# Clearing semaphores on GpSimd after the stage boundary, two sigmoid buffers in the output-maximum pass, and first loads in another order, in a two-layer transformer kernel

## The chip, the cores and the metric

The kernel runs on one core of a Trainium2 chip. The metric is the device time of one execution in microseconds (us). TensorE is called PE in the profile, VectorE DVE, ScalarE ACT, GpSimd POOL and SyncE SP. SP computes nothing here; it issues most of the transfers.

## The reference

Input x is 16 batches of 256 tokens of 512 features; ctx is a context of the same shape. All weights are float32. Four blocks follow one another, each as x = x + block(layernorm(x)):

```python
# 1. cross attention, 16 heads of 64: context rows 0..76 and 77..255 are two separate softmaxes
q = xn @ Wq; out = attend(q, txt @ Wk, txt @ Wv) + attend(q, img @ Wk_ip, img @ Wv_ip)
x = x + out @ Wo + bo
# 2. quantized FFN, 512 -> 1536 -> 512; act_qdq needs the largest absolute value of the whole tensor
xq = act_qdq(xn); up = act_qdq(xq @ dq(w_up).T); gate = act_qdq(xq @ dq(w_gate).T)
gate = act_qdq(gate * fixed_qdq_u16(sigmoid(gate)))
x = x + act_qdq(gate * up) @ dq(w_down).T
# 3. one-head attention over the context: both sides go through (v @ W1.T + b1) @ W2.T + b2
x = x + softmax(proj(xn) @ proj(ctx).T / sqrt(512) + mask) @ ctx
# 4. FFN 512 -> 2048 -> 512, each layer with three routed rank-8 LoRA experts, relu between
x = x + mole(relu(mole(xn, 1)), 2)
```

## The kernel before

The matrix products keep float32 accuracy by splitting each operand into a high part (fp32r, written by ACT with a Copy) and a low part (what is left, written by DVE or POOL with a subtraction); `product` issues three matmuls for one (lines L187 to L189).

The program is a row of stages, each one block in which every engine has its own instruction list, ordered by hand and tied by semaphores. The stages, with the name that prefixes their tiles:

- `c0` makes two constants; `pr` projects the context and prepares normalized x.
- `at` is the cross attention over 128 steps (batch and head pair).
- `pg` and `pu` are the gate and up projections of the quantized FFN over 8 chunks of 512 tokens.
- `om` (`output_maximum`) finds the largest absolute value of gate times up, which the last quantization needs. It runs 48 steps n of 1024 columns. Meanwhile PE folds W1 and W2 of block 3 into one Gram matrix and makes the folded keys from the context.
- `dn` (`down`) requantizes and multiplies with w_down, 8 chunks of six steps s.
- `ma` is the masked attention over 16 batches, `lf` the LoRA FFN over 8 chunks.

A stage owns a `Phase`, which hands out tiles and semaphores. When the last engine of a stage has arrived at the barrier at the end of its block, `Phase.__exit__` opens one more block, in which SP clears every semaphore of the phase (L87 to L91), and ends it with a second barrier. The numbers of semaphores are: c0 2, pr 34, at 57, pg 53, pu 29, om 49, dn 16 (and then qf, the phase around pg to dn, 3 in a block of its own), ma 61, lf 35, 339 together.

**Head of at.** ACT first waits for the bias bo and converts it (L932, L933); DVE first waits for that and makes its low part (L852, L853). Only then come their loops, from s = -3: ACT copies the keys (`keys_high`) and the first query projection (`high_parts`, L929), DVE makes the low part (L824), and PE may start the next queries. SP issues the loads of bo after those of xT, k and v.

**om.** DVE's step n is `outputs(n)` (L1665), `products(n + 2)` (L1653), sometimes `context_low` (L1658), and `largest(n)` (L1669); in even steps `rounded` (L1643) comes first. `products` multiplies the gate by its rounded sigmoid `sq`. For even n the sigmoid is computed again by ACT (L1553), for odd n it is loaded from HBM. All loads of `sq` have one buffer, and SP issues them behind the load of raw:

```python
if n >= 2: sp.wait_ge(up_ready, n - 1)
sp.dma_start(raw[:, n % 2, :], ...)
if n % 2:
    if n >= 2: sp.wait_ge(prod_done, n - 1)
    sp.dma_start(sq[:, 1, :], ...)
```

ACT's step n is `products(n)` (up, L1560, and gate, L1562), then side work, among it `context(x)` (L1571), which takes a transposed half chunk of the context, `turn(x)` of PE (L1738), out of PSUM. DVE's `context_low(x)` follows it, and PE's `turn(x + 1)` waits for that. Halves 0 and 1 are done at ACT's n = 3 and 9, DVE's n = 4 and 10; half 2 follows at ACT's n = 15. ACT's `keys` of the first chunk come at n = 16. POOL loads half 2 only after its work on the folded matrices. At the end SP issues five loads of w_down's parts into `wd`, three of them (k 0 to 3, low part, and k 4 to 7, both parts) after the last store of key biases.

**Head of dn.** SP loads the residual of a chunk (`dn_y`, L1822, 1 MB), then raw of step 0, 1 and so on (L1825, 512 KB each). Then ACT makes up (L1850), DVE the product (L1872), ACT oq and the high part (L1853, L1861), DVE the low part (L1874), and PE its first matmul. PE needs `wd` k 4 to 7 from step s = 2 on. POOL stores the results.

**Head of ma.** SP's order is x(0), keys(0), x(1), values(0), mask, the key biases `traw`, and so on. ACT's list has `keys_high(0)`, then a wait for `traw` and its high part (L2174), then `normalized(0)` (L2129), which lets PE start. DVE makes the low part of `traw` (L2113) after `statistics(0)`.

**Head of lf.** POOL clears the tile `zg` in three memsets (L2455 to L2458); DVE and PE begin with `wait_ge(cleared, 3)`. SP loads the first rows of x3, DVE's first work is `stats` (L2473).

Of the kernel before, what the change touches and what calls it, by code (L numbers as in the profile page):

```python
# [23 lines left out]
P = 128  # L24
# [47 lines left out]
class Phase:  # L72


    def __init__(self, nc, name):
        self.nc, self.name, self.ctx = nc, name, ExitStack()
        self.sems, self.blocks = [], ExitStack()
# [25 lines left out]
    def sem(self, name):  # L103
        self.sems.append(self.ctx.enter_context(self.nc.semaphore(f"{self.name}_{name}")))
        return self.sems[-1]
# [17 lines left out]
def kernel_program(nc, a, out):  # L123
# [11 lines left out]
    with ExitStack() as top:  # L135
# [7 lines left out]
        with Phase(nc, "lo") as ph:  # L143
            sides = LoraSides(nc, ph)
            masked_attention(nc, a, ctx_in, keys_d, bias_d, split_d, x2, x3, sides, ident, neghalf)
            lora_ffn(nc, a, sides, x3, out_f, ident, neghalf)

# [81 lines left out]
def cross_attention(nc, a, x_in, ctx_in, x1, xt_d, wg_d, big, scal, ident, neghalf):  # L229
# [3 lines left out]
    with Phase(nc, "xo") as top:  # L233
# [351 lines left out]
def attend_pairs(nc, a, x_in, xn_d, k_d, v_d, x1, xt_d, wq, wo, big, scal, ident, neghalf):  # L585
# [12 lines left out]
    with Phase(nc, "at") as ph:  # L598
# [59 lines left out]
        with nc.Block() as block:  # L658
# [136 lines left out]
            def _(dve):  # L795
# [85 lines left out]
            def _(act):  # L881
# [159 lines left out]
SUB = 6  # L1041
# [125 lines left out]
def quantized_ffn(nc, a, ctx_in, x1, xt_d, wg_d, x2, raw_up, raw_gate, keys_d, bias_d, big, scal, ident, neghalf):  # L1167
# [4 lines left out]
    with Phase(nc, "qf") as top:  # L1172
        with ExitStack() as gates:
            with Phase(nc, "qu") as mid:
                wu = mid.sb("wu", [P, 2, KD, FF], F32R)
                with Phase(nc, "qg") as low:
# [12 lines left out]
            down(nc, x1, x2, raw_up, gate, wd, wd_late, scal, neghalf)  # L1189
# [247 lines left out]
def output_maximum(nc, a, ctx_in, keys_d, bias_d, raw_up, gate, sq_d, big, scal, folds, wd, wd_parts, wd_late, ident):  # L1437
# [9 lines left out]
    with Phase(nc, "om") as ph:  # L1447
# [3 lines left out]
        sq = ph.sb("sq", [P, 2, SC], U16)  # L1451
# [5 lines left out]
        sq_ready, sig_ready, sq_done = ph.sem("sq_ready"), ph.sem("sig_ready"), ph.sem("sq_done")  # L1457
# [49 lines left out]
        with nc.Block() as block:  # L1507
            def place(n):
# [1258 lines left out]
```

## Time and profile before

| | |
|---|---|
| runs | 3504.18 us, median of 3 (3500.18 to 3504.94) |
| profiled execution | 3504.39 us, of which the span from first to last instruction is 3502.7 us |
| mean granted clock of PE | 0.963 of full speed |
| busy, share of the span | PE 92%, DVE 55%, ACT 44%, POOL 22% |
| transfers | 503.48 MB, 144 GB/s mean |

A profile row of the timeline gives the start in us, the duration, the engine (SPq, ACTq: its queue of DMA issues), the line, the operation, output and inputs with their shapes, how many were merged, and in brackets the idle time of the engine before it with what ended it. The row of an issue has the time of issuing, not of the transfer. The semaphore clears themselves have no row: they show as the gap between the last row of a stage and the first of the next.

### The profile page before, as it was taken

The numbers are of one execution on the slowest core, as the hardware profiler recorded it, in microseconds if no ns is written. First come the engines' busy times: TensorE is split into PE (matmuls) and PEld (weight loads), VectorE is DVE, ScalarE is ACT, GpSimd is POOL, SyncE is SP. The second block draws the span as 40 slices with busy tenths as digits, with TensorE's granted clock in tenths as the row PEclk, the third lists the DMA queues.
The fourth block names the chain that finished last, engine by engine and source line by source line (L and its number), as shares of the span: only waits on it lengthen the run. The fifth ranks groups of instructions, "written<-read, shape, count | busy, mean of one in ns | idle before, by whom it ended". The sixth has DMA issues, their size and how long they took to land. (4 is left out here: it accounts for less than half of the span.)

```text
span 3502.7 us, 51565 instructions
## 1 busy us (share of the span) xinstructions
PE 3225.8 (92%) x17304; PEld 2762.2 (79%) x17304; DVE 1919.8 (55%) x3294; ACT 1557.3 (44%) x2948; POOL 779.3 (22%) x1136
## 2 busy tenths in 40 slices
PE   7999979999999979998996787997959999999998
PEld 6989869999999967886885565885847777877776
DVE  3245558888888855556888885554743222122211
ACT  3222257777777743335776775654722111111110
POOL 0000057777777740000000200002710000000000
PEclk9999989999999999999998898998979999999999
DMA  6477754555555426555666675444832100011000
GB/s 184 134 238 235 220 171 148 153 156 165 154 153 159 144 95 243 177 174 174 221 221 218 208 235 200 166 168 148 253 103 84 37 31 19 24 36 37 31 25 12
DMA packets 370165, 503.48 MB, mean 144 GB/s; under 512 B 58940, under 2 KB 237420, under 8 KB 366032
## 3 DMA queue, kind: packets, MB, share of 16 engines
q1 hardware_dynamic: 356746, 475.46, 43.2%
q0 software_dynamic: 4480, 16.78, 1.4%
q10 hardware_dynamic: 8720, 8.41, 0.7%
q8 instruction: 127, 2.08, 0.3%
q14 instruction: 92, 0.75, 0.1%
HBM read 292.86 MB, written 174.11 MB: 133 GB/s over the span
## 5 line engine op out<-in xcount | busy, mean ns | idle before, releaser
L2522 DVE SCALAR_TENSOR_TENSOR lf_hT<-lf_hb,lf_hT 128x512 fp32r<-128x512 f32 x128 | 88.6, 692 | 618.8 <-ACT lf_hT L2587 617.4
L2587 ACT ACTIVATE lf_hT<-lf_hb 128x512 fp32r<-128x512 f32 x128 | 76.8, 600 | 685.1 <-PE lf_py L189 636.4
L770 POOL TENSOR_TENSOR at_prob<-at_prob,at_rec 128x308 f32<-128x308 f32 (+1 forms) x256 | 261.4, 1043 | 199.1 <-DVE at_rec L812 198.9
L906 ACT ACTIVATE at_prob<-at_sc,at_nm 128x77 f32<-128x77 f32 (+1 forms) x1024 | 293.5, 383 | 3.3 <-DVE at_nm L799 3.3
L799 DVE TENSOR_REDUCE at_nm<-at_sc 128x4 f32<-128x308 f32 (+1 forms) x256 | 164.8, 686 | 82.4 <-PE at_sc L960 80.8
L919 ACT ACTIVATE at_pT<-at_tp 128x1024 fp32r<-128x1024 f32 x128 | 131.8, 1030 | 166.7 <-PE at_tp L970 166.6
L187 PE MATMUL lf_hb<-lf_xT,lf_w 128*128 128x512 f32 x512 | 204.8, 400 | 0.0
L189 PE MATMUL lf_hb<-lf_xT,lf_w 128*128 128x512 f32 x512 | 203.7, 398 | 0.0
L189 PE MATMUL lf_py<-lf_w,lf_hT 128*128 128x512 f32 x512 | 203.2, 397 | 0.0
L188 PE MATMUL lf_hb<-lf_xT,lf_w 128*128 128x512 f32 x512 | 203.1, 397 | 0.0
L187 PE MATMUL lf_py<-lf_w,lf_hT 128*128 128x512 f32 x512 | 202.8, 396 | 0.0
L188 PE MATMUL lf_py<-lf_w,lf_hT 128*128 128x512 f32 x512 | 202.3, 395 | 0.0
L187 PE MATMUL dn_py<-qf_wd,dn_om 128*128 128x512 f32 x384 | 150.7, 393 | 25.2 <-DVE dn_om L1874 25.2
L805 DVE TENSOR_REDUCE at_sums<-at_prob 128x4 f32<-128x308 f32 (+1 forms) x256 | 172.9, 676 | 0.0
L816 DVE TENSOR_TENSOR at_pT<-at_tp,at_pT 128x1024 fp32r<-128x1024 f32 x128 | 156.5, 1222 | 29.9 <-ACT at_pT L919 29.9
L187 PE MATMUL pg_bank<-pg_xs,qg_wg 128*128 128x512 f32 x384 | 153.0, 398 | 20.7 <-DVE pg_xs L1369 20.7
L757 POOL TENSOR_TENSOR at_ks<-at_kr,at_ks 128x512 fp32r<-128x512 f32 x128 | 165.3, 1292 | 16.1 <-ACT at_ks L913 16.1
L187 PE MATMUL pu_bank<-pu_xs,qu_wu 128*128 128x512 f32 x384 | 150.8, 393 | 17.4 <-DVE pu_xs L1369 16.9
L2462 POOL TENSOR_SCALAR lf_var<-lf_mv 128x1 f32<-128x1 f32 x32 | 7.1, 223 | 717.4 <-DVE lf_mv L2475 717.4
L187 PE MATMUL at_vq<-at_xT,xo_Wq 128*128 128x256 f32 x512 | 147.0, 287 | 19.3 <-DMA at_xT<-xn_parts 12.7
L187 PE MATMUL at_vq<-at_pT,at_vs 128*128 128x256 f32 x512 | 154.9, 303 | 0.2 <-DVE at_qst L824 0.2
L960 PEld LDWEIGHTS at_sc<-at_ks,at_qs 128*128 128x128 f32 x1024 | 140.4, 192 | 14.2 <-DMA at_qs<-at_qst 4.4
(324 smaller groups left out, 9510.0 us busy)
## 6 DMA issues: line engine op xcount, KB each, us to landing
at_kr<-k_rows SPq DMA_DIRECT2D x256, 128.0 KB, 2.9
at_qs<-at_qst SPq DMA_DIRECT2D x512, 64.0 KB, 2.1
raw_gate<-pg_stage SPq DMA_DIRECT2D x96, 256.0 KB, 2.0
pu_rg<-raw_gate SPq DMA_DIRECT2D x96, 256.0 KB
raw_up<-pu_stage SPq DMA_DIRECT2D x96, 256.0 KB, 2.1
om_raw<-raw_up SPq DMA_DIRECT2D x48, 512.0 KB, 4.3
dn_raw<-raw_up SPq DMA_DIRECT2D x48, 512.0 KB, 3.8
xn_parts<-pr_xturned SPq DMA_DIRECT2D x32, 512.0 KB, 4.8
```

Source lines behind the costliest of these rows:

```text
L187: pe.matmul(out, lh, rh, start=start, stop=False, **kw)
L188: pe.matmul(out, lh, rl, start=False, stop=False, **kw)
L189: return pe.matmul(out, ll, rh, start=False, stop=stop, **kw)
L757: pool.tensor_tensor(ks[:, n % NK, :, 1, :], kr[:, n % NKR], ks[:, n % NK, :, 0, :].bitcast(F32), ALU.subtract).then_inc(k_low, 1)
L770: ins = pool.tensor_tensor(prob[:, i, :, lo:hi], prob[:, i, :, lo:hi], rec[:, z, g, :].unsqueeze(2).broadcast_to([P, 2 * NTE, hi - lo]), A ...
L799: ins = dve.tensor_reduce(nm[:, n % 2, g, :], sc[n % 2][:, :, lo:hi], AX_X, ALU.max, negate=True)
L805: dve.tensor_reduce(sums[:, z, g, :], prob[:, i, :, SEG[g][0]:SEG[g][1]], AX_X, ALU.add).then_inc(sum_done, 1)
L816: dve.tensor_tensor(pT[:, n % 2, 1], tp[:], pT[:, n % 2, 0].bitcast(F32), ALU.subtract).then_inc(pt_done, 1)
L906: ins = act.activation(prob[:, i, m, lo:hi], sc[n % 2][:, m, lo:hi], ACT.Exp, bias=nm[:, n % 2, g, m:m + 1])
L919: act.activation(pT[:, n % 2, 0], tp[:], ACT.Copy).then_inc(pt_hi, 1)
L960: ins = pe.matmul(sc[n % 2][:, h * NTE + m, :], qs[:, n % NQ, h, m * P:(m + 1) * P], ks[:, n % NK, h, part, :], start=part == 0, stop=part ...
L2522: dve.scalar_tensor_tensor(hT[:, i, 1, :], hb[i][:], 0.0, hT[:, i, 0, :].bitcast(F32), ALU.max, ALU.subtract).then_inc(h_done, 1)
```

## The change

Four things are edited.

1. `Phase`: there is no second block. After the barrier of a stage POOL alone gets the clears, ahead of its own list of the next stage, and the other engines go on. The numbers of the semaphores stay taken until the next stage has ended.
2. `om`: `sq` has three buffers, one for even and two for odd n. The load of an odd sq stands ahead of that of raw and waits only for the product four steps back. `turn`, `context` and `context_low` of half 0 move to after PE's beta products, ACT's n = 9 and DVE's n = 10; those of half 1 to after PE's constants, ACT's n = 14 and DVE's n = 15. The load of w_down's k 4 to 7 leaves `om`.
3. `dn`: that load (two of 1 MB) is issued by POOL as soon as raw of step 1 has landed; the residual is loaded after raw of step 1 instead of ahead of step 0.
4. Heads: in `at` bo is converted at s = 0 (ACT) and s = 1 (DVE). In `ma` `traw` is the first load and is split first on ACT and DVE, and its store is issued ahead of the mask.

```diff
     def __exit__(self, *a):
         self.blocks.close()
-        if self.sems:
-            with self.nc.Block() as block:
-                @block.sync
-                def _(sp):
-                    for s in self.sems:
-                        sp.sem_clear(s)
+        if self.leaf:
+            Phase.retired.close()
+        for s in self.sems:
+            self.nc.gpsimd.sem_clear(s)
+        Phase.retired.push(self.sem_ctx.pop_all())
         return self.ctx.__exit__(*a)
...
 # attend_pairs, DVE and ACT
-                dve.wait_ge(bo_high, 1)
-                dve.tensor_tensor(bo[32:64, :], xn[32:64, :], bo[32:64, :].bitcast(F32), ALU.subtract).then_inc(bo_low, 1)
                 for s in range(FIRST, LAST + 1):
+                    if s == 1:
+                        dve.wait_ge(bo_high, 1)
+                        dve.tensor_tensor(bo[32:64, :], xn[32:64, :], bo[32:64, :].bitcast(F32), ALU.subtract).then_inc(bo_low, 1)
...
-                act.wait_ge(bo_ready, 32)
-                act.activation(bo[:], xn[:], ACT.Copy).then_inc(bo_high, 1)
                 for s in range(FIRST, LAST + 1):
+                    if s == 0:
+                        act.wait_ge(bo_ready, 32)
+                        act.activation(bo[:], xn[:], ACT.Copy).then_inc(bo_high, 1)
...
 # output_maximum
-        sq = ph.sb("sq", [P, 2, SC], U16)
+        sq = ph.sb("sq", [P, 3, SC], U16)
...
                 def load_main(n):
+                    if n % 2:
+                        if n >= 4:
+                            sp.wait_ge(prod_done, n - 3)
+                        sp.dma_start(sq[:, place_of(n), :], part(sq_d, n // SUB, n % SUB)).then_inc(sq_ready[n // 2 % 2], 16)
                     if n >= 2:
                         sp.wait_ge(up_ready, n - 1)
                     sp.dma_start(raw[:, n % 2, :], part(raw_up, n // SUB, n % SUB)).then_inc(raw_ready[n % 2], 16)
-                    if n % 2:
-                        if n >= 2:
-                            sp.wait_ge(prod_done, n - 1)
-                        sp.dma_start(sq[:, 1, :], part(sq_d, n // SUB, n % SUB)).then_inc(sq_ready, 16)
...
                 load_down((1,), (0, KD))
-                load_down((0, 1), (KD, 2 * KD))
...
-                    if n == 3:
-                        context(0)
...
                     if n == 9:
...
-                        context(1)
+                        context(0)
...
                         act.activation(bb[:], tb[:, 16:17], ACT.Copy, scale=SCALE).then_inc(gc_out, 1)
+                        context(1)
...
-                    if n == 4:
+                    if n == 10:
                         context_low(0)
-                    if n == 10:
+                    if n == 15:
                         context_low(1)
...
 # down
-                        sp.wait_ge(y_free, 2 * it + par + 1)
-                        sp.dma_start(y[:, par], tokens(x1, 2 * it + par)).then_inc(res_ready[par], 16)
                         for s in range(SUB):
                             sp.wait_ge(up_ready, 2 * SUB * it + SUB * par + s + 1)
                             sp.dma_start(raw[:, s % 2, :], part(raw_up, 2 * it + par, s)).then_inc(raw_ready[s % 2], 16)
+                            if s == 1:
+                                sp.wait_ge(y_free, 2 * it + par + 1)
+                                sp.dma_start(y[:, par], tokens(x1, 2 * it + par)).then_inc(res_ready[par], 16)
...
+                pool.wait_ge(raw_ready[1], 16)
+                for h in range(2):
+                    pool.dma_start(wd[:, h, KD:2 * KD, :].bitcast(F32), wd_parts[:, h, KD:2 * KD, :].bitcast(F32)).then_inc(wd_late[1], 16)
...
 # masked_attention, SP
+            sp.dma_start(traw[:], bias_d.rearrange("c (b s) -> (c b) s", b=NB)).then_inc(traw_ready, 16)
             load_x(0)
             load_keys(0)
             load_x(1)
             load_values(0)
+            sp.wait_ge(t_low, 1)
+            sp.dma_start(split_d, tsplit[:].bitcast(F32)).then_inc(t_stored, 16)
             sp.dma_start(mask[:], a["fside_1xSxS2_0"].rearrange("o (m p) s -> p (o m) s", p=P)).then_inc(m_ready, 16)
-            sp.dma_start(traw[:], bias_d.rearrange("c (b s) -> (c b) s", b=NB)).then_inc(traw_ready, 16)
```

## Rows read from the trace of the kernel before

**Rows 1.** Busy us (and count) of PE, PEld, DVE, ACT, POOL; clock; DMA share; GB/s.

```profile
452.80:1299.20 846.40, 817.64 (x6048) 772.54 (x6048) 662.86 (x1218) 587.48 (x1601) 609.17 (x931) 0.99 0.50 150
1887.20:2125.10 237.90, 180.20 (x760) 136.82 (x760) 204.43 (x190) 173.21 (x191) 30.70 (x32) 0.86 0.72 226
```

**Rows 2.** Timeline, last and first rows around two boundaries.

```profile
1.59 0.29 POOL L159 TENSOR_SCALAR_AFFINE_SELECT ident<-ident 128x128 f32<-128x128 f32 x1 [0.50 <-POOL ident L157]
2.73 0.44 SPq L358 DMA_DIRECT2D pr_rows<-in_ctx_dram  x1
...
1884.68 0.21 DVE L1209 TENSOR_SCALAR scal<-scal 128x1 f32<-128x1 f32 x1
1887.21 0.34 SPq L1516 DMA_DIRECT2D om_raw<-raw_up  x1
```

**Rows 3.** Timeline, head of at.

```profile
462.67 0.63 ACT L933 ACTIVATE at_bo<-at_xn 128x512 fp32r<-128x512 f32 x1 [19.40 <-DMA at_xn<-in_L_xattn_bo_dram]
...
463.72 0.36 ACT L929 ACTIVATE at_qst<-at_vq 128x256 fp32r<-128x256 f32 x1
...
464.60 0.39 PE L187 MATMUL at_vq<-at_xT,xo_Wq 128*128 128x256 f32 x1 [3.64 <-DVE at_qst L824]
```

**Rows 4.** Waits of DVE in om: us in total, times, longest.

```profile
DVE om_prod L1653 <- DMA om_sq<-gate_sigmoids: 27.1, 12, 10.1
```

**Rows 5.** Timeline of om: its head, and the steps 15 and 16.

```profile
1900.65 1.23 DVE L1653 TENSOR_TENSOR om_prod<-qf_gate,om_sq 128x1024 f32<-128x1024 int16 x1 [10.11 <-DMA om_sq<-gate_sigmoids]
...
1965.32 1.23 DVE L1665 TENSOR_TENSOR om_outp<-qf_gate,om_up 128x1024 f32<-128x1024 int16 x1
...
1970.44 1.23 DVE L1665 TENSOR_TENSOR om_outp<-qf_gate,om_up 128x1024 f32<-128x1024 int16 x1 [1.03 <-ACT qf_gate L1562]
...
1967.31 1.02 ACT L1571 ACTIVATE qf_wd<-om_ctp 128x1024 fp32r<-128x1024 f32 x1 [4.33 <-PE om_ctp L1738]
...
1965.33 1.94 PE L1738 MATMUL om_ctp<-ident,om_cin 128*128 128x128 f32 x8 [18.45 <-issue]
```

**Rows 6.** Timeline, boundary from om to dn.

```profile
2129.48 0.40 SPq L1822 DMA_DIRECT2D dn_y<-x  x1
2130.15 15.52 SPq L1825 DMA_DIRECT2D dn_raw<-raw_up  x4
2139.38 1.15 ACT L1850 ACTIVATE dn_up<-dn_raw,scal 128x1024 int16<-128x1024 f32 x1 [18.35 <-DMA dn_raw<-raw_up]
...
2145.54 0.79 PE L187 MATMUL dn_py<-qf_wd,dn_om 128*128 128x512 f32 x1 [25.22 <-DVE dn_om L1874]
```

**Rows 7.** Landing times of the tiles dn_raw, then qf_wd.

```profile
DMA to landing us min/median/max: 3.5/3.8/9.7
...
DMA to landing us min/median/max: 4.7/7.5/9.6
```

**Rows 8.** Windows of dn, columns as in the first group.

```profile
2145.50:2151.50 6.00, 5.96 (x15) 4.66 (x16) 3.40 (x3) 3.44 (x4) 0.00 (x0) 0.52 0.39 96
2151.50:2409.20 257.70, 257.70 (x1138) 213.38 (x1137) 129.48 (x122) 148.47 (x137) 5.48 (x7) 1.00 0.43 147
```

**Rows 9.** Timeline, head of ma.

```profile
2425.49 0.20 POOL L2035 TENSOR_TENSOR ma_shift<-ma_minus,ma_rstd 128x2 f32<-128x2 f32 x1
...
2427.35 0.42 ACT L2174 ACTIVATE ma_tsplit<-ma_traw 16x256 fp32r<-16x256 f32 x1 [2.56 <-DMA ma_traw<-key_biases]
2427.67 1.51 ACT L2129 ACTIVATE ma_xn<-ma_y,ma_shift,ma_rstd 128x512 f32<-128x512 f32 x2
```

**Rows 10.** Timeline, head of lf.

```profile
2581.08 0.53 POOL L2455 MEMSET lf_zg<- 128x512 f32 x1 [27.99 <-POOLq L87]
...
2581.66 0.10 POOL L2457 MEMSET lf_zg<- 128x4 f32 x1
2581.70 0.11 POOL L2458 MEMSET lf_zg<- 128x4 f32 x1
...
2584.05 0.69 DVE L2473 BATCH_NORM_STATS2 lf_st<-lf_xin 128x6 f32<-128x512 f32 x1 [10.11 <-DMA lf_xin<-x]
```

More of the change, by code:

```diff
@@ L72, with __init__ @@
 class Phase:
-    def __init__(self, nc, name):
-        self.nc, self.name, self.ctx = nc, name, ExitStack()
+    retired = ExitStack()
+    def __init__(self, nc, name, leaf=True):
+        self.nc, self.name, self.leaf, self.ctx, self.sem_ctx = nc, name, leaf, ExitStack(), ExitStack()
         self.sems, self.blocks = [], ExitStack()
@@ L103, in sem @@
     def sem(self, name):
-        self.sems.append(self.ctx.enter_context(self.nc.semaphore(f"{self.name}_{name}")))
+        self.sems.append(self.sem_ctx.enter_context(self.nc.semaphore(f"{self.name}_{name}")))
         return self.sems[-1]
@@ L142, in kernel_program @@
         quantized_ffn(nc, a, ctx_in, x1, xt_d, wg_d, x2, raw_up, raw_gate, keys_d, bias_d, big, scal, ident, neghalf)
-        with Phase(nc, "lo") as ph:
+        with Phase(nc, "lo", leaf=False) as ph:
             sides = LoraSides(nc, ph)
@@ L146, in kernel_program @@
             lora_ffn(nc, a, sides, x3, out_f, ident, neghalf)
+    Phase.retired.close()
 def consts(nc, ident, neghalf):
@@ L232, in cross_attention @@
     v_d = nc.dram_tensor("v_rows", (TOK, INNER), F32).ap()
-    with Phase(nc, "xo") as top:
+    with Phase(nc, "xo", leaf=False) as top:
         wq = top.sb("Wq", [P, 2, KD * INNER], F32R)
@@ L1170, in quantized_ffn @@
     sq_d = nc.dram_tensor("gate_sigmoids", (NCH, P, KF * CT), U16).ap()
-    with Phase(nc, "qf") as top:
+    with Phase(nc, "qf", leaf=False) as top:
         with ExitStack() as gates:
-            with Phase(nc, "qu") as mid:
+            with Phase(nc, "qu", leaf=False) as mid:
                 wu = mid.sb("wu", [P, 2, KD, FF], F32R)
-                with Phase(nc, "qg") as low:
+                with Phase(nc, "qg", leaf=False) as low:
                     wg = low.sb("wg", [P, KF, 2, KD, P], F32R)
@@ L1456, in output_maximum @@
         raw_ready = [ph.sem(f"raw_ready{i}") for i in range(2)]
-        sq_ready, sig_ready, sq_done = ph.sem("sq_ready"), ph.sem("sig_ready"), ph.sem("sq_done")
+        sq_ready = [ph.sem(f"sq_ready{i}") for i in range(2)]
+        sig_ready, sq_done = ph.sem("sig_ready"), ph.sem("sq_done")
         up_ready, prod_done, gate_ready, out_done, max_done = (
@@ L1507, in output_maximum, with place_of @@
         with nc.Block() as block:
+            def place_of(n):
+                return 1 + n // 2 % 2 if n % 2 else 0
             def place(n):
@@ L1647, in products @@
                     if s:
-                        dve.wait_ge(sq_ready, 16 * (n // 2) + 16)
+                        dve.wait_ge(sq_ready[n // 2 % 2], 16 * (n // 4) + 16)
                     else:
@@ L1652, in products @@
                         dve.wait_ge(gate_ready, n - 1)
-                    dve.tensor_tensor(prod[:, s, :], place(n), sq[:, s, :], ALU.mult).then_inc(prod_done, 1)
+                    dve.tensor_tensor(prod[:, s, :], place(n), sq[:, place_of(n), :], ALU.mult).then_inc(prod_done, 1)
                 def context_low(x):
@@ L1746, in _ @@
                     ins.then_inc(turned, 1)
-                turn(0)
                 pe.wait_ge(w1_ready, 16)
@@ L1758, in _ @@
                 ins.then_inc(beta_full, 1)
-                turn(1)
+                turn(0)
                 pe.wait_ge(m_out, KD)
@@ L1771, in _ @@
                 ins.then_inc(gc_full, 1)
+                turn(1)
                 pe.wait_ge(gram_low, KD)
@@ L1793, in _, with down @@
                     ins.then_inc(t_full, 1)
-def down(nc, x1, x2, raw_up, gate, wd, wd_late, scal, neghalf):
+def down(nc, x1, x2, raw_up, gate, wd, wd_parts, wd_late, scal, neghalf):
     NO = 3
@@ L2102, in outputs @@
                     dve.scalar_tensor_tensor(y[:, b % NX, t, :], po[:, t, :], rec[:, b % 2, t:t + 1], y[:, b % NX, t, :], ALU.mult, ALU.add).then_inc(y_done, 1)
+            dve.wait_ge(t_high, 1)
+            dve.tensor_tensor(tsplit[:, 1, :], traw[:], tsplit[:, 0, :].bitcast(F32), ALU.subtract).then_inc(t_low, 1)
             for s in range(FIRST, LAST + 1):
@@ L2110, in _ @@
                     statistics(s + 3)
-                if s == FIRST:
-                    dve.wait_ge(t_high, 1)
-                    dve.tensor_tensor(tsplit[:, 1, :], traw[:], tsplit[:, 0, :].bitcast(F32), ALU.subtract).then_inc(t_low, 1)
                 if 0 <= s < B:
@@ L2165, in turned_high @@
                 act.activation(pT[:, b % 2, 0], tp[b % 2][:], ACT.Copy).then_inc(pt_high, 1)
+            act.wait_ge(traw_ready, 16)
+            act.activation(tsplit[:, 0, :], traw[:], ACT.Copy).then_inc(t_high, 1)
             for s in range(FIRST, LAST + 1):
@@ L2171, in _ @@
                     keys_high(s + 2)
-                if s == FIRST + 1:
-                    act.wait_ge(traw_ready, 16)
-                    act.activation(tsplit[:, 0, :], traw[:], ACT.Copy).then_inc(t_high, 1)
                 if 0 <= s + 1 < B:
```

4 lines of the change are left out of this document (1 added, 3 removed).

## The prediction

> **What bounds the kernel now.** I read the page first: PE is busy 92% of the span, every other engine much less. That is an average over stages, so the second view is the table of busy time by stage. In the attention stage PE is busy 817.6 of 846.4 us, so nothing inside its loop can give much, only its head. The output-maximum stage om is another case: DVE is busy 204.4 of 237.9 us, PE 180.2, ACT 173.2 [rows 1]. There DVE sets the pace, and the view of waits says what it misses: 27.1 us in 12 waits, all for the loaded sigmoids, the longest 10.1 us at the head, so 17.0 us in 11 waits later [rows 4]. The third view is the timeline at each boundary between stages, where no engine computes and every microsecond is on the path. The gap from the last row to the first of the next stage is 2.73 - 1.88 = 0.85 us after c0 with 2 semaphores, and 1887.21 - 1884.89 = 2.32 us after pu with 29 [rows 2]. The difference, 1.47 us for 27 more clears, is 0.054 us each; I use 0.055. What is left of 0.85 after two clears, 0.74, is two block exits, 0.37 each.
>
> **Part 1, the clears.** On SP all 339 are on the path. Leaving out ma and lf, which are special, 2 + 34 + 57 + 53 + 29 + 49 + 19 = 243 clears go, 13.4 us, and 8 second exits (qf has its own), 3.0 us: 16.3 us in all (rounded once). The cover is POOL's idle time at the head of each stage. POOL's next work is not on the path after c0, pg, at and dn; after pr it clears tiles for which SP asks late; after pu it issues a context load that PE needs only at n = 9 now. Clears on POOL have no row. Bounds for one: 0.04 us, two memsets in a row at 2581.66 and 2581.70, and 0.11 us, the duration of the shorter kind [rows 10]. I take 0.07, between them and a little above SP's.
>
> After ma POOL is on the path. DVE and PE of lf wait for its memsets, which take from 2581.08 to 2581.81, 0.7 us. The barrier would release at 2581.08 - 61 x 0.055 - 0.37 - about 0.2 = 2577.1; then 61 x 0.07 = 4.3 us of clears and 0.7 of memsets end at 2582.1, while the rows of x, loaded 3.7 us earlier, have landed at about 2580.3. DVE starts at 2582.1 instead of 2584.05 [rows 10]: 1.9 us, between 3.7 (0.04 each) and 0. At the end of the program 35 clears only change engine: 35 x 0.015 = 0.5 us lost and 0.37 won, nothing.
>
> **Part 2, om.** The wait for sq comes from its place: it is issued behind raw, which waits for ACT's up two steps back. Now it is issued about one step earlier, more than the longest but two of the later waits need. Bounds: none of the 17.0 us, if ACT or PE becomes the bound, or all. DVE's busy time leaves room for all (237.9 - 204.4 = 33.5 idle), PE has 57 us of idle. The load of 1 MB at n = 24 still stands in front of one sq. I take 80%, 13.5 us. At the head sq of step 1 now goes ahead of raw of step 1; 512 KB at the stage's 226 GB/s [rows 1] is 2.3 us, and ACT needs raw too, so I take 1.7, between 0 and 2.3.
>
> The moved context half costs. PE's transpose of half 2 must wait for DVE's low part of half 1, which now stands in step 15. DVE has one such operation less ahead of it, so `outputs(15)` comes 1.2 us earlier, at 1964.1; it, `products(17)` and the low part take 3.45 us, to 1967.6. PE's transposes at this slow clock take 1.9, to 1969.5, where ACT had started its copy at 1967.31 and DVE's `outputs(16)` had already waited 1.03 us for what ACT does behind it [rows 5]. So step 16 is 2.2 us late. The low bound of this loss is 0, if POOL's load of half 2 was late anyway by as much (the bracket of PE's row says it was ready just then); the high one 3.5. om gains 13.5 + 1.7 - 2.2 = 13.0 us.
>
> **Part 3, dn.** Raw of step 0 was issued at 2130.15, used at 2139.38: 9.2 us, where the median load of this tile lands in 3.8 [rows 6, 7]. In front of it stood three loads of w_down and the residual. Two of the three and the residual go, so it lands in 3.8: 5.4 us; and the issue of the residual, 2130.15 - 2129.48 = 0.67 us, is no longer ahead. From ACT's first row PE follows 6.2 us later as before, and is busy without a break until 2409.2 [rows 6, 8], so the 6.1 us are kept. What is late next? The two loads on POOL. With R the issue of raw 0, raw 1 has landed at about R + 4.2. PE starts at R + 10.0. Its steps 0 and 1 are 48 matmuls: 15 in 6.0 us at a granted clock of 0.52, 33 at 257.7 / 1138 = 0.226 us [rows 8], 13.5 us, so w_down's second third is needed at R + 23.5. Loads of this kind landed in 7.5 us, 9.6 at worst [rows 7]: side by side R + 12 to 14, one after the other at worst R + 23.4. Hidden, with nothing to spare in the worst case. Raw 2 shares the engines with 3 MB, but is needed only 5 us and more after it is asked for.
>
> **Part 4, heads.** In at PE's first group ended at 464.60 - 3.64 = 460.96. ACT copied the query at 463.72 because the bias came first, at 462.67 [rows 3]. It could start at 461.0: 2.7 us at most. The copies of the bias, 0.63 and 0.68 us, now fall into the filling loop, where ACT and DVE are less covered; I take 2.2, between 0 and 2.7. In ma the start of `normalized(0)` was 2427.67, behind the split of traw, though its shift was ready at 2425.69 [rows 9]. Now traw is long there; but its issue stands ahead of x(0), 0.47 us. So beyond the boundary's 1.9 us the head gains 2427.67 - 2425.69 - 0.47 = 1.5, bounds 0 and 2.0; I take 1.4.
>
> **Sum.** 16.3 + 1.9 (lf) + 13.0 + 6.1 + 2.2 + 1.4 = 40.9 us. From the profiled execution's 3504.4, which stands 0.2 above the median of the runs, that gives 3463.5, so 3464.
>
> **Rivals.** A: the wait in om only changes its name. ACT is busy 173 us and waits for PE's transposes besides [rows 1, 5]; if that loop sets the pace once sq is there, only 4 of the 13.5 us come: 3473. For it: ACT's row at 1967.31 waited 4.33 us for PE. Against it: DVE hardly waits for ACT now, and both others are less busy than DVE.
>
> B: the loads on POOL come late, and PE stalls at s = 2 of the first chunk. It decides from R + 23.5 on. If they need 30 us, the loss is 6.5 us: 3470. For it: 3 MB are under way at once. Against it: the rows of landing above.
> On this the Trainium skill speaks against the change (DMA: Bandwidth & Descriptors, SWDGE vs HWDGE vs iDMA): GpSimd writes its descriptors into SBUF itself, and VectorE locks it out there in its two-port mode, while transfers from SP are immune. No row here shows such a lockout. By the same page's fit (Anatomy of one DMA) a load of 1 MB takes an estimated 4.4 us, and this rival would be dead.
>
> C: the gap at a boundary is not the clears but transfers and the barrier. Then part 1 gives only the exits, 3 us, and the sum is 27: 3477. Against it: the gap grows with the number of semaphores at a steady rate.
>
> D, slower: a clear on POOL is dear, and POOL holds back the heads. Its place is lf (61 ahead of the memsets), the end (35) and at (34 ahead of the clearing of xn, which SP asks for about 5 us in). With c us each the change loses 61c - 6.25 in lf, 35c - 2.3 at the end and 34c - 5 in at, against 39 us won elsewhere; it turns at c = 0.4. At 0.5 it loses 13 us: 3517. Against it: ten times what the rows of small POOL operations show.
>
> **Chances.** The sum as it stands, 3455 to 3468: 0.62. A 0.17, B 0.08, C 0.04, D 0.03. Better than the sum, 3448 to 3455, if om gives all and the heads their upper bounds (3.5 + 2.2 + 0.6 + 0.5 + 1.8 us more): 0.06. The range 3453 to 3480 takes in A, B and C's better part and most of the bounds: the low ones together would give some 30 us less, but not all at once. A difference of 0.2%, 7 us, is about what a measurement of this kernel can tell from none. Faster 0.95, same 0.02, slower 0.03.
>
> **What the profile after would show.** The gap after c0, pr, at, pg, pu and om is about 0.5 us whatever the number of semaphores, and DVE's first row of lf comes 5 us after the last store's landing at most. The waits for sq in om fall from 27 to under 12 us, with one wait of 2 to 3 us more at step 16. ACT's first row of dn comes about 4 us after the issue of raw, and PE has no idle time in dn behind its first row. PE's second group in at starts within 1 us of the end of the first. The prediction is wrong if ACT's or PE's waits in om grow by what DVE's lose, if PE stalls about 13.5 us into dn, or if POOL's first rows come late by more than 0.1 us a semaphore.

## The result, and the profile after

The changed kernel takes 3467.47 us, the median of 4 runs (3466.56 to 3467.89), where the one before takes 3503.55 beside it: 36.1 us less, a ratio of 0.9899 (95% interval 0.9884 to 0.9915). Forecast were 3464 and 40.2 us less than the first median. The profiled execution took 3467.41 us with a span of 3465.7. Two executions stand far off the others of their kernel, one of the sigmoid buffers alone further down (4520.73 us at a mean granted clock of 0.67, the one whose profile was taken) and one of the kernel before beside it (9628.20 us); they are in no time and no ratio below.

The rows answer to those of before, view by view. First the busy table of the stages at and om, with the columns of [rows 1]:

```profile
456.60:1297.80 841.20, 816.53 (x6048) 771.91 (x6048) 664.27 (x1219) 586.57 (x1601) 610.25 (x932) 0.99 0.51 150
...
1876.80:2099.30 222.50, 176.01 (x760) 132.93 (x760) 203.00 (x186) 172.48 (x191) 32.22 (x32) 0.87 0.74 242
```

In om DVE has the same 203 us of work, in 222.5 us. The stretch of om in [rows 1] ends 1.0 us behind its last reduction; cut like this one it is 236.9 us long, so 14.4 us are gone.

The timeline around the first boundary and that from pu to om, as in [rows 2]:

```profile
1.60 0.29 POOL L162 TENSOR_SCALAR_AFFINE_SELECT ident<-ident 128x128 f32<-128x128 f32 x1 [0.50 <-POOL ident L160]
...
2.37 1.84 SPq L361 DMA_DIRECT2D pr_rows<-in_ctx_dram  x5
...
1876.03 0.21 DVE L1214 TENSOR_SCALAR scal<-scal 128x1 f32<-128x1 f32 x1
1876.73 0.34 SPq L1529 DMA_DIRECT2D om_raw<-raw_up  x1
```

Both gaps are now 0.48 and 0.49 us, with 2 semaphores and with 29: where no store is under way, the gap no longer depends on the number.

The view of waits for om, DVE, which answers to [rows 4], and three rows of the timeline at steps 15 and 16, which answer to [rows 5]:

```profile
DVE om_prod L1660 <- DMA om_sq<-gate_sigmoids: 9.7, 2, 8.5
...
DVE om_outp L1672 <- ACT qf_gate L1570: 4.6, 2, 3.5
```

```profile
1955.99 1.94 PE L1745 MATMUL om_ctp<-ident,om_cin 128*128 128x128 f32 x8 [15.20 <-DVE qf_wd L1665]
...
1957.96 1.02 ACT L1579 ACTIVATE qf_wd<-om_ctp 128x1024 fp32r<-128x1024 f32 x1 [7.97 <-PE om_ctp L1745]
...
1961.10 1.23 DVE L1672 TENSOR_TENSOR om_outp<-qf_gate,om_up 128x1024 f32<-128x1024 int16 x1 [3.53 <-ACT qf_gate L1570]
```

Of the waits for sq 1.2 us are left behind the head. The moved context half shows as a chain: PE's transpose waits for DVE's low part, ACT waits 7.97 us for PE, and DVE 3.53 us for ACT, where it had waited 1.03.

The head of dn (timeline), which answers to [rows 6], and the landing times of dn_raw and then of qf_wd, as in [rows 7]:

```profile
2101.31 0.95 SPq L1830 DMA_DIRECT2D dn_raw<-raw_up  x2
...
2105.47 1.15 ACT L1861 ACTIVATE dn_up<-dn_raw,scal 128x1024 int16<-128x1024 f32 x1 [9.22 <-DMA dn_raw<-raw_up]
...
2106.90 1.28 POOL L1839 DMA_DIRECT2D qf_wd<-wd_parts  x2 [7.69 <-DMA dn_raw<-raw_up]
...
2111.63 0.79 PE L190 MATMUL dn_py<-qf_wd,dn_om 128*128 128x512 f32 x1 [16.09 <-DVE dn_om L1885]
```

```profile
DMA to landing us min/median/max: 3.5/3.8/7.2
...
DMA to landing us min/median/max: 7.7/9.1/10.5
```

Raw of step 0 is used 4.2 us after its issue instead of 9.2. POOL's two loads land 7.7 and 10.5 us after theirs, the last of them at about 2118; by the working of rival B PE needs it at 2101.3 + 23.5 = 2124.8. In the table of windows PE has no idle time there, as before it [rows 8]:

```profile
2111.70:2117.70 6.00, 6.00 (x16) 4.72 (x17) 3.28 (x3) 3.54 (x4) 0.00 (x0) 0.55 0.98 371
2117.70:2375.60 257.90, 257.87 (x1138) 213.20 (x1136) 129.49 (x122) 148.26 (x137) 6.07 (x8) 1.00 0.45 146
```

Last the three other heads, from the timeline; they answer to [rows 3, 9, 10]:

```profile
459.08 0.58 PE L190 MATMUL at_vq<-at_xT,xo_Wq 128*128 128x256 f32 x1 [11.67 <-DMA at_xT<-xn_parts]
...
462.05 0.38 ACT L933 ACTIVATE at_qst<-at_vq 128x256 fp32r<-128x256 f32 x1 [0.72 <-PE at_vq L192]
...
462.95 0.58 PE L190 MATMUL at_vq<-at_xT,xo_Wq 128*128 128x256 f32 x1 [0.94 <-DVE at_qst L827]
...
2384.63 0.42 ACT L2178 ACTIVATE ma_tsplit<-ma_traw 16x256 fp32r<-16x256 f32 x1 [23.72 <-DMA ma_traw<-key_biases]
...
2390.51 0.20 POOL L2046 TENSOR_TENSOR ma_shift<-ma_minus,ma_rstd 128x2 f32<-128x2 f32 x1
...
2390.83 1.52 ACT L2139 ACTIVATE ma_xn<-ma_y,ma_shift,ma_rstd 128x512 f32<-128x512 f32 x2 [1.07 <-POOL ma_shift L2046]
```

```profile
2540.81 0.83 SPq L2421 DMA_DIRECT2D lf_xin<-x  x2
...
2545.31 0.53 POOL L2464 MEMSET lf_zg<- 128x512 f32 x1 [29.00 <-issue]
...
2546.06 0.69 DVE L2482 BATCH_NORM_STATS2 lf_st<-lf_xin 128x6 f32<-128x512 f32 x1 [8.91 <-POOL lf_zg L2467]
```

In at PE waits 0.94 us between its first two groups instead of 3.64. In ma ACT normalizes at once when the shift is there. In lf DVE now waits for POOL, whose memsets start 4.5 us after SP's first issue, behind 61 clears.

### The profile page after: what moved, and what is told of

Same layout as the page of the kernel before. It is cut to its first block and busy times, and to the rows that moved or that the text cites. A ratio compares the mean times of both kernels' runs of the same rounds, so it can differ in the third digit from the quotient of the medians.

```text
span 3465.7 us, 51456 instructions
## 1 busy us (share of the span) xinstructions
PE 3221.9 (93%) x17304; PEld 2759.2 (80%) x17304; DVE 1922.2 (55%) x3294; ACT 1554.9 (45%) x2948; POOL 781.9 (23%) x1138
## 5 line engine op out<-in xcount | busy, mean ns | idle before, releaser
L190 PE MATMUL pg_bank<-pg_xs,qg_wg 128*128 128x512 f32 x384 | 153.2, 399 | 16.4 <-DVE pg_xs L1374 16.4
L760 POOL TENSOR_TENSOR at_ks<-at_kr,at_ks 128x512 fp32r<-128x512 f32 x128 | 165.8, 1296 | 11.3 <-ACT at_ks L917 11.3
L191 PE MATMUL pg_bank<-pg_xs,qg_wg 128*128 128x512 f32 x384 | 150.8, 393 | 0.0
```

Source lines behind the costliest of these rows:

```text
L190: pe.matmul(out, lh, rh, start=start, stop=False, **kw)
L191: pe.matmul(out, lh, rl, start=False, stop=False, **kw)
L760: pool.tensor_tensor(ks[:, n % NK, :, 1, :], kr[:, n % NKR], ks[:, n % NK, :, 0, :].bitcast(F32), ALU.subtract).then_inc(k_low, 1)
```

## The experiments

Each kernel was timed beside the one before, on the same chip within a group. The profile of each is one execution, so the stretches are compared over all of them. In the tables of this section "PE's part" of a stage is the time from PE's first row in it to its last.

**The clears alone**, edit 1 on the kernel before.

```diff
-                    for s in self.sems:
-                        sp.sem_clear(s)
+        for s in self.sems:
+            self.nc.gpsimd.sem_clear(s)
```

> The kernel before with the clears alone moved to GpSimd. My theory (the clears and the second exits are on the path, and POOL's clears are covered everywhere but in front of lf): 16.3 + 1.9 = 18.2 us faster than before, each gap between stages shorter by 0.055 us a semaphore and some 0.4 for the exit, lf by about 1.2 to 1.9. Rival C (the gap is transfers and barrier): some 3 us only. Rival D (dear clears): slower. Where the head of at or a projection's first loads become late because SP's clears had covered something, a boundary's gain is missing at PE's first matmul, although it is there at the first issue.

Measured: 3484.11 us against 3500.8, ratio 0.9947 (0.9934 to 0.9961), so 16.7 us by the medians and 18.6 by the ratio (13.7 to 23.1). Rivals C and D are out. With 13 profiles the boundaries can be averaged: five with the clears on SP (before, and the kernels below with edit 3 alone, the heads alone, the buffers alone and the load behind raw) and eight with the clears on POOL. The time from the start of PE's last row of a stage to SP's first issue of the next, in us:

```
into      semaphores  on SP   on POOL   gain   by 0.055 each + 0.37 an exit
at            34       7.92     6.82    1.10      2.24
pg            57       9.37     5.57    3.80      3.51
pu            53       9.50     5.93    3.56      3.29
om            29      12.39    10.55    1.83      1.96
dn            49       9.85     6.21    3.65      3.06
ma         16 + 3      9.11     7.72    1.39      1.78
```

With 0.36 us after c0 (2.73 - 2.37) that is 15.7 us, forecast 16.3. Only the boundary into at misses a whole microsecond. The trace holds the start of each clear and of each wait of SP, though no view prints them, and there the two parts come apart. From the release of the barrier to SP's first issue in at it takes 2.27 us with the clears on SP and 0.08 with them on POOL: 2.19 of the 2.24 are there. But SP arrives at the barrier 3.9 to 4.3 us behind its last issue of pr in the five executions, and 5.0 to 5.5 in the eight, since before that it waits for pr's last stores to land. Why they land 1.1 us later is open.

The same starts show what a clear takes: they stand 0.055 us apart on SP, with one pause of 0.39 us into pg and one of 0.38 into dn, and 0.071 apart on POOL, with one pause each of 0.36 to 0.44 us into at, pg and lf. In the kernel with the clears alone too, DVE's first row of lf waits for POOL:

```profile
2563.70 0.84 SPq L2415 DMA_DIRECT2D lf_xin<-x  x2
...
2568.20 0.53 POOL L2458 MEMSET lf_zg<- 128x512 f32 x1 [29.05 <-issue]
...
2568.96 0.69 DVE L2476 BATCH_NORM_STATS2 lf_st<-lf_xin 128x6 f32<-128x512 f32 x1 [8.95 <-POOL lf_zg L2461]
```

**The sigmoid buffers alone.**

```diff
-        sq = ph.sb("sq", [P, 2, SC], U16)
+        sq = ph.sb("sq", [P, 3, SC], U16)
...
                 def load_main(n):
+                    if n % 2:
+                        if n >= 4:
+                            sp.wait_ge(prod_done, n - 3)
+                        sp.dma_start(sq[:, place_of(n), :], ...)
```

> The kernel before with the two buffers for the loaded sigmoids and their load ahead of raw, and nothing else: the context halves stay at n = 3 and 9, all loads of w_down stay in om. My theory: om is shorter by 17 us or a little less (the changed kernel's om became 14.4 us shorter, and its move of the context halves cost some 2.5 of what the buffers gave); 15 to 17 us faster than before. Rival: the move of the halves cost nothing, and this kernel gains 14.4 or less.

Measured: 3487.92 us against 3500.8, ratio 0.9964 (0.9951 to 0.9978), 12.9 us by the medians and 12.6 by the ratio. The 15 to 17 expected are missed. By the number the rival's 14.4 or less came, but its reason, that the move of the halves cost nothing, falls further down; the 17 us were those of one execution. The kernel was run once more, for a profile of the stage.

> The kernel before with the two sigmoid buffers alone, once more, since the first profile of it was taken at a clock of 0.67. Three profiles of om as it stood before show PE's part of it 223.7, 218.2 and 218.3 us long, with 17.0, 11.2 and 11.3 us of DVE's waits for sq behind the head. My theory: this kernel's waits for sq fall to 1 or 2 us behind the head, and PE's part is 208 to 210 us long, some 9 to 10 below 218.3 and as short as in the changed kernel with the halves back. 11 to 13 us faster than before.

Measured: 3490.77 us against 3501.34, ratio 0.9968 (0.9956 to 0.9980), 10.6 us by the medians, where 11 to 13 were expected. PE's part of om is 209.1 us, as expected. DVE's waits for sq in om, 2.4 us of them behind the head:

```profile
DVE om_prod L1657 <- DMA om_sq<-gate_sigmoids: 10.4, 3, 8.0
```

**Two buffers, but the load behind raw.**

```diff
                     if n >= 2:
                         sp.wait_ge(up_ready, n - 1)
                     sp.dma_start(raw[:, n % 2, :], ...)
+                    if n % 2:
+                        if n >= 4:
+                            sp.wait_ge(prod_done, n - 3)
+                        sp.dma_start(sq[:, place_of(n), :], ...)
```

> As the last, but the load of sq stands behind that of raw, as before; it still waits only for the product four steps back. The step of my prediction: the wait came from the place, behind raw, which waits for ACT's up two steps back. By it most of the wait stays: 7 us or more behind the head, and a gain of 4 us or less. Rival: the one buffer made the wait (the load could start only after the product two steps back), and the place is worth only the head's 1.6 us: waits of 1 to 3 us behind the head, 9 to 12 us faster than before.

Measured: 3499.02 us against 3501.34, ratio 0.9996 (0.9987 to 1.0005): no gain that can be told.

```profile
DVE om_prod L1657 <- DMA om_sq<-gate_sigmoids: 22.2, 12, 9.9
```

Behind the head 22.2 - 9.9 = 12.3 us remain, as much as without the second buffer. The place in SP's list made the wait, as the prediction's step said, and the rival falls: a second buffer alone gives nothing. That it is needed at all, so that the load can stand in the better place, is argued; one buffer with the load in front of raw was not run.

**The w_down load and the residual alone**, edit 3 on the kernel before.

```diff
-                load_down((0, 1), (KD, 2 * KD))
...
+                            if s == 1:
+                                sp.wait_ge(y_free, 2 * it + par + 1)
+                                sp.dma_start(y[:, par], ...)
...
+                pool.wait_ge(raw_ready[1], 16)
+                for h in range(2):
+                    pool.dma_start(wd[:, h, KD:2 * KD, :], ...)
```

> The kernel before with the last load of w_down on POOL in dn and the residual behind raw of step 1, nothing else. My theory: 6 us faster, ACT's first row of dn about 4.2 us after the issue of raw instead of 9.2, no idle time of PE in dn behind its first matmul. Rival B: PE stalls at s = 2 and the gain is below 3 us.

Measured: 3496.01 us against 3500.8, ratio 0.9991 (0.9982 to 1.0000), so 3.2 us by the ratio and 4.8 by the medians, where 6 were expected; the interval reaches from 0 to 6 us, and the profiles have to say the rest. The timeline of the head of dn:

```profile
2124.42 0.95 SPq L1822 DMA_DIRECT2D dn_raw<-raw_up  x2
...
2128.38 1.15 ACT L1853 ACTIVATE dn_up<-dn_raw,scal 128x1024 int16<-128x1024 f32 x1 [12.84 <-DMA dn_raw<-raw_up]
```

4.0 us of latency, as in the changed kernel, and no idle time of PE in dn. But the latency of before is no constant: in the five executions that kept the old order it is 9.2, 9.9, 8.0, 6.8 and 8.3 us, 8.4 on average. The 9.2 that the sum used was on the high side. From PE's last row of om to its first of dn this kernel has 20.1 us, the four others with this boundary 23.5 to 25.6, mean 24.7: 4.6 us. From SP's first issue in dn to PE's first row it is 15.3 us on average in the five executions with the old order (13.6 to 16.8) and 10.3 in the seven with the new one and w_down's loads in time: 5.0 us, from 3.4 to 6.5 by the execution.

**The heads alone**, edit 4 on the kernel before.

```diff
-                act.wait_ge(bo_ready, 32)
-                act.activation(bo[:], xn[:], ACT.Copy).then_inc(bo_high, 1)
                 for s in range(FIRST, LAST + 1):
+                    if s == 0:
+                        act.wait_ge(bo_ready, 32)
+                        act.activation(bo[:], xn[:], ACT.Copy).then_inc(bo_high, 1)
...
+            act.wait_ge(traw_ready, 16)
+            act.activation(tsplit[:, 0, :], traw[:], ACT.Copy).then_inc(t_high, 1)
             for s in range(FIRST, LAST + 1):
```

> The kernel before with the bias converted inside the loop in at and the key biases split first in ma, nothing else. My theory: PE's 40th matmul of at comes 2.2 us earlier, PE's first matmul of ma 1.4 us earlier, 3.6 us faster than before in all. Rival: the start of at is bound by something behind the head (the queries' stacking, the loads of x), so that the 2.2 us are given back within 50 us, and the whole gain is 1.4 to 2 us. A further 3 us at the first batch's end, as the changed kernel shows, would be the effect of this edit if it comes here, and chance or the boundary's if it does not.

Measured: 3496.21 us against 3500.8, ratio 0.9984 (0.9975 to 0.9993), 4.6 us by the medians and 5.6 by the ratio (2.5 to 8.8), expected 3.6. From SP's first issue in at to PE's 40th matmul the five executions with the old head take 17.0 to 18.9 us, mean 18.0, and this one 16.35; to the 200th, 42.5 against 41.3. So 1.7 us are won and 1.2 stay. From PE's end of dn to its first row of ma: 18.7 us against 20.2 in the four with the same boundary.

**The changed kernel once more.**

> The changed kernel itself once more, as the base of the next three. 35 to 37 us faster than before. It also asks what of its profile was chance: PE's 480th matmul of at came 77.2 us after the stage's first load in the changed kernel's profile, and 81.2 to 82.4 in four profiles without the whole change. If that is the two edits together, it comes again here and in the next three; if it was chance, some of the four are near 82.

Measured: 3467.16 us against 3501.41, ratio 0.9909 (0.9894 to 0.9924), 34.3 us by the medians, a little under the 35 to 37 expected. PE's 480th matmul of at comes 77.4 us after the first issue, again early. In the five other kernels that have the clears on POOL and the new head together it comes at 81.5, 78.7, 80.6, 81.0 and 78.4, in the six that lack one of the two or both at 81.2 to 83.9. The view of waits, from 485 to 520 us, of the changed kernel and then of the next one below, with the halves back, says what the difference is:

```profile
PE at_sc L965 <- DMA at_qs<-at_qst: 1.1, 1, 1.1
```

```profile
PE at_sc L965 <- DMA at_qs<-at_qst: 3.3, 1, 3.3
```

PE waits there for the stacked query, a small transfer, for 0.5 to 6.4 us, and this changes between executions of the same code. That it is shorter on average with the change (seven executions against six, 79.3 against 82.5, of which the head's 1.2 us are a part) looks real, but what makes it so stays open.

**The context halves back at n = 3 and 9** (edit 2 without its moves).

```diff
+                    if n == 3:
+                        context(0)
...
                     if n == 9:
-                        context(0)
+                        context(1)
...
-                        context(1)
```

> The changed kernel with the two context halves back at n = 3 and 9, 4 and 10. My theory: the halves' move makes DVE wait 3.5 us at step 16 where it waited 1.0, and ACT 8.0; without it om is shorter by about 2.5 us and the kernel 2 to 3 us faster than the changed one. Rival: the early halves make another wait (POOL's load of half 2 or PE's folding of W1 and W2, which the transposes then stand in front of), and the time is the same or slower.

Measured: 3465.22 us against 3501.41, ratio 0.9898 (0.9882 to 0.9913), 1.9 us below the changed kernel of the same group by medians of four, whose runs overlap (3462.80 to 3465.51 against 3463.16 to 3471.40). DVE's wait for ACT in om:

```profile
DVE om_outp L1673 <- ACT qf_gate L1570: 1.9, 2, 1.1
```

4.6 us in two waits have become 1.9. PE's part of om over all profiles:

```
old loads of sq, halves at 3 and 9            223.7  220.6  218.2  218.3 (and 219.2, load behind raw)
new loads, halves moved (the changed kernel)  211.7  212.9  211.8  212.3  211.4
new loads, halves at 3 and 9                  209.1  209.3  208.9
```

The move costs 2.9 us, the difference of the means 212.0 and 209.1. The new place of the load gives 9 to 15 us, by the execution that it is compared with, 11.1 against the mean of the four, 220.2. DVE sets the pace of om, not PE; counted from SP's first issue instead, the three means are 228.3, 218.8 and 216.8 us, so 2.1 us for the move and 11.5 for the place.

**Every semaphore cleared twice.**

```diff
         for s in self.sems:
             self.nc.gpsimd.sem_clear(s)
+            self.nc.gpsimd.sem_clear(s)
```

> The changed kernel with every semaphore cleared twice on GpSimd: 339 more clears of 0.071 us, 24 us of POOL's time. My theory: they are covered everywhere but in front of lf (61, 4.3 us) and at the end (35, 2.5 us), so 6.8 us slower than the changed kernel, perhaps 1 more in om, where the first context load stands behind them. Rival: POOL's clears are not covered at the other heads (at, dn), up to 24 us slower.

Measured: 3475.14 us against 3501.41, ratio 0.9919 (0.9905 to 0.9932): 8.0 us above the changed kernel of the group, expected 6.8 and perhaps 1 more. PE's first row of lf stands 18.31 us behind its last of ma, where the changed kernel has 14.01, 4.30 us for 61 clears: 0.0705 us each. At the other boundaries the gap to PE's first row differs from the changed kernel's by 0.4 us or less. The cover holds where it was claimed; only lf and the end pay.

**The clears where they cost nothing** (the halves back, besides).

```diff
         for i, s in enumerate(self.sems):
+            if self.name == "ma":
+                nc.scalar.sem_clear(s)
+            elif self.name == "lf":
+                (nc.gpsimd, nc.sync, nc.scalar, nc.vector, nc.tensor)[i % 5].sem_clear(s)
```

> The kernel with the halves back, and ma's 61 clears on ACT, which has no work in lf before its first transposed rows, and lf's 35 at the end spread over the five engines. If an ACT clear costs 0.05 to 0.08 us: DVE's first row of lf about 1.8 us earlier (the rows' own landing then decides), the end some 2 us earlier, 3 to 4 us faster than the kernel with the halves back. Rival: another engine's clear is dearer than POOL's, and lf's first ACT row comes late.

Measured: 3459.61 us against 3501.41, ratio 0.9878 (0.9863 to 0.9893). That is 7.6 us below the changed kernel and 5.6 below the one with the halves back, by medians of four; the fastest version of the study. The head of lf:

```profile
2538.73 0.53 POOL L2471 MEMSET lf_zg<- 128x512 f32 x1 [24.38 <-POOLq L88]
2538.87 0.83 SPq L2428 DMA_DIRECT2D lf_xin<-x  x2
...
2541.67 0.69 DVE L2489 BATCH_NORM_STATS2 lf_st<-lf_xin 128x6 f32<-128x512 f32 x1 [6.47 <-DMA lf_xin<-x]
```

DVE starts 2.8 us after SP's issue instead of 5.25, released by the rows themselves. So 2.4 us were left in this head. The last 35 clears take 0.9 us from the first to the end, on POOL 2.5. Together that is 4.0 us, the upper end of the 3 to 4 expected; the rest of the 5.6 may be spread, since the four runs lie 8.6 us apart.

**The residual first again.**

```diff
                     for par in range(2):
+                        sp.wait_ge(y_free, 2 * it + par + 1)
+                        sp.dma_start(y[:, par], ...)
                         for s in range(SUB):
...
-                            if s == 1:
-                                sp.wait_ge(y_free, 2 * it + par + 1)
-                                sp.dma_start(y[:, par], ...)
```

> The changed kernel with the residual's load ahead of each chunk's raw again; w_down's part still comes on POOL. The head of dn gained 5 us of latency of raw 0 and 0.5 to 0.7 us of issue. The residual is 1 MB of the 3 MB that went: if bytes in front decide, a third to a half of the 5 us goes back, and with it the issue: 2.3 to 3.2 us slower than the changed kernel. Rival: the loads of w_down alone had been in the way: only the issue, 0.5 to 0.7 us.

Measured: 3469.74 us against 3501.34, ratio 0.9914 (0.9900 to 0.9927). The timeline:

```profile
2100.50 0.40 SPq L1829 DMA_DIRECT2D dn_y<-x  x1
2101.17 22.22 SPq L1832 DMA_DIRECT2D dn_raw<-raw_up  x6
...
2107.60 1.15 ACT L1860 ACTIVATE dn_up<-dn_raw,scal 128x1024 int16<-128x1024 f32 x1 [12.15 <-DMA dn_raw<-raw_up]
```

6.43 us of latency instead of 4.16, and 0.67 us of issue: 2.9 us for one load of 1 MB in front, about what 1 MB takes at the 371 GB/s that the profile shows in dn's first 6 us (2.8 us). Bytes in front decide.

**w_down's loads later.**

```diff
-                pool.wait_ge(raw_ready[1], 16)
+                pool.wait_ge(raw_ready[0], 48)
```

> The changed kernel with POOL's two loads of w_down held until raw of step 4 has landed (in the changed kernel: step 1). By rival B's working w_down's second third is needed 23.5 us after the issue of raw 0, and the loads landed 7.7 and 10.5 us after theirs. Raw of step 4 is issued about 15 us after raw 0 and lands at about 19; so the loads land at 28 to 30 and PE stalls 5 to 6.5 us behind its first 48 matmuls. If it stalls by that, the slack of the changed kernel is 23.5 less the landing of its loads, some 6 us, and rival B was a matter of 6 us.

Measured: 3472.77 us against 3501.34, ratio 0.9922 (0.9907 to 0.9937). POOL issued them at 2118.66, 18.9 us after raw 0. The timeline of PE, and the table of windows around the stall:

```profile
2122.17 0.39 PE L192 MATMUL dn_py<-qf_wd,dn_om 128*128 128x512 f32 x1
2127.94 0.77 PE L190 MATMUL dn_py<-qf_wd,dn_om 128*128 128x512 f32 x1 [5.38 <-DMA qf_wd<-wd_parts]
```

```profile
2115.90:2122.50 6.60, 6.60 (x30) 5.18 (x28) 2.36 (x2) 4.99 (x5) 1.38 (x3) 1.00 0.57 190
2122.50:2127.90 5.40, 0.06 (x1) 0.00 (x0) 2.65 (x3) 3.90 (x5) 0.00 (x0) 0.89 1.00 399
2127.90:2130.90 3.00, 2.96 (x7) 2.41 (x8) 2.08 (x2) 1.61 (x2) 0.00 (x0) 0.50 0.56 158
2130.90:2133.90 3.00, 3.00 (x9) 2.32 (x9) 0.00 (x0) 0.26 (x1) 0.59 (x1) 0.56 0.92 295
```

PE stalls 5.38 us, in the range expected. It ends its first 48 matmuls 22.8 us after the issue of raw 0, in place of the 23.5 worked out. The loads of the changed kernel landed at 2118 and were needed by about 2124, so its slack is some 6 us. Rival B was this close. Its price is more than the stall: PE's part of dn is 270.6 us instead of 263.5, 7.1 more, since the clock granted after the stall is 0.50 and 0.56, 1.2 GHz for most of 6 us, as at a stage's head.

## Why the prediction was right

The time lies in the range, 3.5 us above the value, and the gain is 90% of the one forecast. The shown terms add up to 34.3 us. The edits alone, by the medians of their kernels, give 16.7, 10.6 to 12.9, 4.8 and 4.6 us, and the move of the halves takes 1.9 of that: 34.8 to 37.1 together. Point by point, predicted and shown:

```
term                         predicted   shown
clears, exits, without lf       16.3     15.7   mean of 5 against 8 boundaries each
head of lf                       1.9      1.1   14.01 against 15.13 from PE to PE
om: new place of the load       15.2     11.1   220.2 against 209.1, from 9 to 15 by execution
om: context halves moved        -2.2     -2.9   212.0 against 209.1
dn                               6.1      4.6   24.7 against 20.1; 5.0 from SP's first issue on
head of at                       2.2      1.2 kept of 1.7
head of ma                       1.4      1.5   18.7 against 20.2
rest of at                       0        2     open
```

- **The clears.** SP's 0.055 us and POOL's 0.07 a clear held (0.071 by the starts in the trace, 0.0705 by the doubled clears). The exit's 0.37 did not: it halves 0.74 us that were thought to be two exits, but 0.48 us are left after c0 with one, so the exit that went was worth 0.85 - 0.11 - 0.48 = 0.26. That is 0.9 us too much over eight exits, and into at 1.1 us are missing, since pr's last stores land later. Against that, SP's pauses into pg and dn went with the clears, and into pu SP had one of 0.39 us in front of its first issue that went too; the slope of 0.055 holds none of them. So 15.7 beside 16.3 is in part luck: three errors nearly cancel. Wrong was also the sentence that the gap after c0, pr, at, pg, pu and om is 0.5 us: it is so only where no store is on its way; after pg it takes 2.6 us from DVE's last row to SP's first issue. For the gain this doesn't matter, since the stores' landing stood in both, with at as the exception.
- **lf.** The mechanism held, POOL is the one that is waited for, but 1.1 us came of 1.9. SP's first clear before, at 2577.51, shows the barrier released at about 2577.4 instead of 2577.1, and POOL's 61 clears with a pause take 4.7 us from the first to the memset (2540.63 to 2545.31) instead of 4.3.
- **om.** The mechanism was right and shown by the load put back behind raw: that kernel gains nothing. The size was off. The term that was mis-sized is "behind the head 17.0 us of waits": the profiled execution had an expensive om. Three others of the same code show 12.2, 11.3 and 11.2 us of these waits and a PE's part 3 to 5.5 us shorter. The 80% that I took then gave 13.5 us where some 9.5 were to be had on average (11.1 less the head's 1.6). The later waits are also gone more fully than 80%: 1.2 us of them are left.
- **The context halves** cost about what the rows of [rows 5] gave (2.2 forecast, 2.1 to 2.9 shown): DVE's wait of 3.53 us where 1.03 + 2.2 = 3.2 was worked out. The lower bound, no loss because POOL's load would be late anyway, is out.
- **dn.** Raw lands in 4.2 us, 3.8 was taken; PE runs without a break. Again the single execution was a little dear (9.2 us against a mean of 8.4). The residual is worth 2.9 us of it; that w_down's two loads are the rest is a difference and was not run alone.
- **The heads.** ma's term held. Of at's 2.2 some was given back before the 200th matmul, as the rival of that experiment had it in part. That the total is near the forecast all the same owes something to the 2 us or so by which PE's wait for the stacked queries was shorter, which no step foresaw.
- **Rivals.** A fell: DVE's longest wait for ACT grew by 2.5 us, through the halves and not through ACT's load. B had 6 us of slack. On its sentence from the Trainium skill (DMA: Bandwidth & Descriptors, SWDGE vs HWDGE vs iDMA), that VectorE locks GpSimd's descriptor writes out in its two-port mode: POOL's two issues together took 1.28 us in the changed kernel and in the others, and no row shows one held up. DVE was busy beside them, but with a product, and no run here shows in which mode that ran, so the sentence was not put to the test. By the fit of the Trainium skill (the same page, Anatomy of one DMA) a load of 1 MB takes an estimated 4.4 us; measured were 7.7 and 10.5 in the changed kernel (the prediction had 9.6 as the worst), with raw and the residual under way at the same time. C and D fell with the first experiment and with the doubled clears.

## What to carry to other kernels

A block that only cleans up costs its instructions and a second barrier on every engine's path; put its work at the head of an engine that has nothing to do there, and look boundary by boundary for the one where that engine is the first to be waited for. A second buffer is worth nothing while its load still stands behind a waiting instruction in its queue: the place in the list is the change. And a stage whose waits are for transfers should be read in more than one execution before its waits are counted as gain: here one profile showed 17 us of waits where three others showed 11 to 12.

## What the runs showed of the hardware

- Semaphore clears start 0.055 us apart on SP, 0.071 on POOL and 0.066 on ACT, where nothing pauses them. Single pauses of 0.35 to 0.44 us among them come at the same boundaries in every execution with the same clears. The second exit after c0 cost 0.26 us.
- The same instructions up to the end of pr ended at times up to 6.6 us apart: SP's first issue in at came at 449.7 to 456.3 us in the profiles, while the kernels differ by 1.1 us at the boundary ahead of it. A median of runs averages this, one profile doesn't.
- A stall of 5.4 us in the middle of a dense stretch cost 7.1, since the granted clock fell from 1.00 to 0.50, and PE's matmuls of 512 columns went from 0.39 to 0.63 us until the clock was back about 5 us later.
- In om a DVE product of 1024 columns takes 1.22 us, but 1.6 to 2.3 us in a few rows near 1940 us of the changed kernel's profile. What shares its path there was not tested.
